# A shifted-window attention block: the value projection over all 128 rows in two column tiles, the output projection 128 columns wide

## The chip, the cores and the metric

The kernel runs on one core of one Trainium2 chip. The metric is device microseconds of one execution, start to end. A run of the program is timed as a whole; the profile is one further execution under the hardware profiler.

## What is computed

One Swin block on an input of 32 x 56 x 56 pixels with C = 64 channels, 8 heads of D = 8, windows of 7 x 7 = 49 tokens, shifted by 3:

```python
y = roll(layernorm(x), (-3, -3)); win = windows(y)                # (2048, 49, 64)
q, k, v = (win @ qkv_w.T).reshape(..., 3, 8, 8)
attn = softmax(q @ k.T * D**-0.5 + bias[head] + mask)
out = (attn @ v) @ proj_w.T + proj_b                              # per window
x = x + roll(windows_back(out), (3, 3))
x = x + gelu(layernorm(x) @ fc1_w.T + fc1_b) @ fc2_w.T + fc2_b    # hidden 256
```

The relative-position bias is made on the chip once, from a small network; everything is float32 at the boundary.

## The kernel before, in words

**Units.** The image is cut into 128 super-blocks (`NSB`). One holds 16 windows: 8 positions along the free axis (`UP`), each with two windows, one on partitions 0 to 48 and one on 64 to 112 (`W0 = 64`, `R = 113`). A round of the pipeline, `body(i)`, works on one super-block at each stage: while the scores of block i are made, block i+1 gets its projections, block i-1 its output projection, block i-3 its hidden layer, and so on.

**The order.** There is no scheduler. Each engine has its own `body(i, m)`, and the order in it is written by hand. Semaphores tie them. A round on TensorE has eight steps k = 0 to 7. Each step has the same core: `scores` (line 723, with 727 where a mask applies), `scores_T` (739), `shift` (745) and `times_v` (759). One extra piece is put between `scores_T` and `shift` (or at the end of the step):

- k = 0: `turn_back` (862), then `project_qk` (785)
- k = 1: `project_v` (801)
- k = 2 and 3: the two halves of `fc1` (832)
- k = 4: `turn_y` (767), then `fc2` (854)
- k = 5: `turn_o` (767); k = 6: `project_out` (818); k = 7: `turn_z` (767)

VectorE, ScalarE and GpSimd run their loops as a hardware loop of four rounds. TensorE's program is written out in full for all 135 rounds (`for i in range(-3, NSB + 4)` at its end), so it is one long straight piece of code.

**Operands.** `yT` holds the normalised tokens transposed: partitions 0 to 63 are the 64 channels of the even positions, 64 to 127 those of the odd ones (index h). The weights lie in both halves (`twice`), so that each half of the rows has its own copy. `M` is four PSUM banks of 512 float32 columns.

**`project_v(u)`** (line 796) makes 32 matmuls: for each of 8 token groups s, for both row halves h and both head parities e, stationary `yT[64 rows, 49 columns]`, moving `wv[64 rows, 32 columns]`. The four go to four quarters of the array, `tile_position=(C * h, W0 * e)`, and write bank 2 + h. A float32 matmul is executed as two MATMULs with two weight loads, so the trace counts 64. ScalarE's `place_v` (line 421, activation at 428) copies both banks into `vx`, the ring of values that `times_v` reads by a window index (line 756).

**`project_out(u, f)`** (line 811) makes 8 matmuls: for each q of 4 and each row half h, stationary `oT[64 rows, 113 columns]`, moving `wproj[64 rows, 64 columns]`, output bank h. VectorE's `add_attention` (606, 610) adds both banks to the residual.

**Start.** VectorE fills the PSUM tiles S, ST and O (505 to 507); TensorE waits for these three (`BLANK`, line 693), and then for the constants' chain on VectorE.

Of the kernel before, what the change touches and what calls it, by code (L numbers as in the profile page):

```python
# [14 lines left out]
N = WIN * WIN  # L15
SHIFT = 3
HEADS = 8
D = 8
C = HEADS * D
HID = 4 * C  # L20
PAIRS = 4
W0 = 64
R = W0 + N
# [11 lines left out]
EPS = 1e-5  # L35
U = 8
NVEC = 23 + SPAN
NWT = 768
RING = 4
LAG = 4  # L40
FIRST = 7
# [2 lines left out]
def swin_block(nc, x, c_vec, c_weights, c_projb, c_keys, c_diag, c_shift, out):  # L44
    NSB = x.shape[0]
    ctx = ExitStack()
    with ctx:
        def sb(name, shape, dt=F32):
            return ctx.enter_context(nc.sbuf_tensor(name, shape, dt))

        def ps(name, shape):
            return ctx.enter_context(nc.psum_tensor(name, shape, F32))

        def sem(name):
            return ctx.enter_context(nc.semaphore(name))

        vec = sb("vec", [128, NVEC])
        weights = sb("weights", [128, NWT])
        diag = sb("diag", [RM, 2 * 4, N], F16)
# [8 lines left out]
        line = vec[:, 23:23 + SPAN]  # L68
        ident = weights[:, 0:128]
        wqk = weights[:, 128:256]  # L70
        wproj = weights[:, 256:320]
        w1 = weights[:, 320:576]
        wv = weights[:, 576:640].rearrange("c (e f) -> c e f", e=2)
        w2 = weights[:, 640:768].rearrange("k (a c) -> k a c", a=2)

        st = sb("st", [128, 12, 4])
        tab = sb("tab", [128, 8, SPAN])
# [18 lines left out]
        yT = sb("yT", [2 * C, UT // 2])  # L96
# [3 lines left out]
        vx = [sb(f"vx{r}", [R, 16, 4, VC]) for r in range(RING)]  # L100
# [3 lines left out]
        pT = [sb(f"pT{n}", [R, 2, 4, N]) for n in range(LAG)]  # L104
        rec = sb("rec", [R, 4 * PAIRS, 2])
        on = sb("on", [R, UP, C])
        oT = sb("oT", [2 * C, 4, R])
# [19 lines left out]
        M = ps("M", [128, 4, 512])  # L127
# [6 lines left out]
        c_blank = sem("c_blank")  # L134
# [56 lines left out]
        s_out = [sem(f"s_out{r}") for r in range(2)]  # L191

        ZEROED = RING + 2
        BLANK = 3
        VALUES = 3 * RING

        C_EXP, C_BASE, C_HID = 2, 10, 19
# [1 line left out]
        def on_chip(u):  # L199
            return not isinstance(u, int) or 0 <= u < NSB  # L200

        def later(u, k=1):
            return not isinstance(u, int) or u >= k
# [191 lines left out]
        def _(act):  # L395
# [25 lines left out]
            def place_v(u, r):  # L421
                act.wait_ge(s_vp, u + 1)
                if not later(u, RING):
                    act.wait_ge(c_values, 3 * u + 3)
                dst = vx[r % RING][:].rearrange("n s h f -> n (s h) f")
                for e in range(2):
                    rows = slice(W0 * e, W0 * e + N)
                    nc.scalar.activation(dst[rows, :, D * e:D * e + D].rearrange("n (a s) d -> n a s d", a=2),  # L428
                                         M[rows, 2:4, 0:256].rearrange("n a (s d) -> n a s d", d=D),
                                         ACT.Copy).then_inc(s_vx, 1)  # L430

            def exp(u, j):
# [33 lines left out]
            def body(i, m):  # L466
                a, n, c, d, e = i + 1, i + 3, i - 1, i - 2, i - 3
                if isinstance(i, int) and i == 0:
                    place_bias(0, 1)
                    act.wait_ge(c_zero, ZEROED)  # L470
                for k in range(U):
                    if isinstance(i, int) and i == 0 and k in (5, 7):
                        place_bias(1, k // 7)
                    if k == 0 and on_chip(a):
                        high_parts(a)
                    if k == 1 and on_chip(a):
                        place_v(a, m + 1)
                    u, j = at_unit(i, k, 2)
                    if on_chip(u):
                        exp(u, j)  # L480
                    if k == 0 and on_chip(d):
                        square2(d)
                    if k == 2 and on_chip(e):
                        gelu(e, 0)
                        gelu(e, 1)
                    if k == 3 and on_chip(n):
                        square1(n)
                    if k == 4 and on_chip(c):
                        evac_oT(c)
                    if k == 5 and on_chip(e):  # L490
                        evac_m(e)
# [4 lines left out]
        def _(dve):  # L496
# [7 lines left out]
            V = nc.vector  # L504
            V.memset(S[:], -1.0).then_inc(c_blank, 1)
            V.memset(ST[:], 0.0).then_inc(c_blank, 1)
            V.memset(O[:], 1.0).then_inc(c_blank, 1)
            dve.wait_ge(c_vec_in, 16)

            then(V.scalar_tensor_tensor(st[:, 0, 0:3], scal[:, 0:3], -1.0, scal[:, 0:3], ALU.mult, ALU.max))  # L510
# [95 lines left out]
            def add_attention(u, r):  # L606
                dve.wait_ge(s_pj, u + 1)
                dve.wait_ge(s_xres, u + 1)
                held = xres[r % RING][:].rearrange("r (p h) c -> r p h c", h=2)
                V.tensor_tensor(held, M[0:R, 0:2, 0:4 * C].rearrange("r h (p c) -> r p h c", c=C), held,  # L610
                                ALU.add).then_inc(s_att, 1)

            def ln2_sum(u, r):
# [33 lines left out]
            def body(i, m):  # L647
# [5 lines left out]
                for k in range(U):  # L653
# [29 lines left out]
                    if k == 6 and on_chip(c):  # L683
                        add_attention(c, m + 3)
# [4 lines left out]
        def _(pe):  # L689
            MM = nc.tensor.matmul  # L690

            pe.wait_ge(c_vec_in, 16)
            pe.wait_ge(c_blank, BLANK)
            pe.wait_ge(c_chain, C_HID)
            for n in range(HALF + 1):
                for half in range(2):
                    kr, kc = divmod(HALF * half + n if n else 0, WIN)
                    dst = S[:] if n < 10 else ST[:, n // 10 - 1, :]
                    mm = MM(dst[W0 * half:W0 * half + HEADS, N * (n % 10):N * (n % 10) + N], cpbw2,
                            hidden[:, kr:kr + WIN, kc:kc + WIN], start=True, stop=True, tile_position=(0, W0 * half))  # L700
# [48 lines left out]
            def times_v(u, r, j):  # L749
                p = j % 4  # L750
                pe.wait_ge(s_e, U * u + j + 1)
                if j == 0:
                    pe.wait_ge(s_vx, 2 * u + 2)
                if p == 0 and (later(u) or j == 4):
                    pe.wait_ge(s_on, 2 * u + j // 4)
                window = 8 * (j % 2) + 4 * (j // 4) + 2 * ((j % 4) // 2)
                for hp in range(4):
                    for w in range(2):
                        mm = MM(O[W0 * w:W0 * w + N, (4 * p + hp) * VC:(4 * p + hp + 1) * VC],  # L759
                                pT[j % LAG][:, w, hp, :], vx[r % RING][:, window + w, hp, :],  # L760
                                start=True, stop=True, tile_position=(0, W0 * w))
                mm.then_inc(s_pv, 1)

# [31 lines left out]

            def project_v(u):
                for s in range(8):
                    for h in range(2):
                        for e in range(2):
                            rows = slice(C * h, C * h + C)  # L800
                            mm = MM(M[W0 * e:W0 * e + N, 2 + h, 32 * s:32 * s + 32], yT[rows, N * s:N * s + N],  # L801
                                    wv[rows, e, :], start=True, stop=True, tile_position=(C * h, W0 * e))
                mm.then_inc(s_vp, 1)

            def turn_o(u, e, a):
# [5 lines left out]
            def project_out(u, f):  # L811
                pe.wait_ge(s_oT, u + 1)
                if on_chip(f):
                    pe.wait_ge(s_yT, f + 1)
                for q in range(4):
                    for h in range(2):
                        rows = slice(C * h, C * h + C)
                        mm = MM(M[0:R, h, C * q:C * q + C], oT[rows, q, :], wproj[rows, :], start=True, stop=True)  # L818
                mm.then_inc(s_pj, 1)

            def turn_z(u, e, a):
# [44 lines left out]
            def body(i, m):  # L866
# [6 lines left out]
                for k in range(U):  # L873
# [14 lines left out]
                    if k == 1 and on_chip(a):  # L888
                        project_v(a)
# [8 lines left out]
                    if k == 6 and on_chip(c):  # L898
                        project_out(c, f)
# [4 lines left out]
                    if on_chip(u4):  # L904
                        times_v(u4, r4, j4)
# [87 lines left out]
```

## Time and profile before

| | |
|---|---|
| median of 3 runs | 2359.13 us (2358.63 to 2376.8) |
| the profiled execution | 2345.75 us, of which the span of the instructions is 2343.9 us |
| TensorE busy (matmul) | 2217.1 us, 95% of the span |
| mean granted TensorE clock | 0.986 |
| rounds | 128 full ones |

How to read it: in the lines of a group, "M<-weights,yT 64*49 64x32 f32" is a MATMUL that writes M, with a stationary operand of 64 rows by 49 columns and a moving one of 64 rows by 32 columns. PE is TensorE's matmul side, PEld its weight loads, which run beside it. Matmuls are pipelined: their durations overlap, so the time that a group takes is read from its start to the start of the next group. "[0.39 <-issue]" is idle time that nothing in the profile released: no semaphore that another engine set late. All starts are microseconds from the first instruction.

### The profile page before, as it was taken

The page shows a single profiled execution, that of the slowest core. Times are in us where ns is not written, and L with a number is a line of the kernel's source. Part 1 is how long each engine was busy: PE and PEld are TensorE (multiplying, and loading weights), DVE is VectorE, ACT ScalarE, POOL GpSimd, SP SyncE. Part 2 cuts the span into 40 slices and gives each one's busy share as a digit, 9 for nine tenths or more (in the row PEclk, how much of TensorE's full clock was granted, in tenths as well). Part 3 has the DMA queues.
Part 4 walks back from the last instruction along what each step waited for, and adds up shares of the span by engine and source line. Part 5 has one row for each costly group of instructions (what it writes and reads, how often), then busy time and mean ns, then how long its engine had stood idle before and what let it go on. Part 6 is the DMA issues. An engine that isn't in the chain of part 4 may idle for free.

```text
span 2343.9 us, 155989 instructions
## 1 busy us (share of the span) xinstructions
PE 2217.1 (95%) x66852; PEld 1699.0 (72%) x66852; DVE 1756.3 (75%) x3230; ACT 1548.0 (66%) x2435; POOL 1770.1 (76%) x1687
## 2 busy tenths in 40 slices
PE   5999999999999999999999999999999999999997
PEld 4777777777777777777777777777677777777775
DVE  5787787777777877777777777777777777777774
ACT  4567666666666776766666766666666666666765
POOL 5787787777777877776777777777777777777774
PEclk7999999999999999999999999999999999999999
DMA  5444444444444454444444444444444444444541
GB/s 122 98 92 103 91 94 100 87 90 90 95 97 90 96 100 90 99 90 85 96 87 92 102 89 93 103 93 90 94 90 89 93 91 97 94 91 93 103 87 41
DMA packets 137659, 217.73 MB, mean 93 GB/s; under 512 B 29336, under 2 KB 95114, under 8 KB 137114
## 3 DMA queue, kind: packets, MB, share of 16 engines
q1 hardware_dynamic: 137114, 208.95, 43.2%
q8 instruction: 527, 8.63, 1.7%
q14 instruction: 18, 0.15, 0.0%
HBM read 131.69 MB, written 77.15 MB: 89 GB/s over the span
## 4 chain that ended last, share of the span: by engine, by line
PE 85%; ACT 6%; issue 5%; DMA 1%; DVE 1%; POOL 0%; SPq 0%; ACTq 0%; POOLq 0%; DVEq 0%
PE O L759 13%; PE ST L745 11%; PE S L723 9%; PE M L767 9%; PE ST L739 8%; PE M L832 7%; PE M L854 7%; PE M L818 5%; PE M L785 5%; PE M L801 5%; PE M L862 3%; ACT L456 3%; ACT gl L456 2%; PE S L727 2%; DMA xin<-in_x 0%
## 5 line engine op out<-in xcount | busy, mean ns | idle before, releaser
L337 POOL TENSOR_TENSOR nmd<-diag,nm 121x392 f16<-121x392 f16 x1024 | 897.4, 885 | 435.6 <-DVE nm L592 412.5
L592 DVE TENSOR_REDUCE nm<-S 121x8 f16<-121x392 f32 x1024 | 576.7, 563 | 375.9 <-PE S L727 185.0
L437 ACT ACTIVATE pT<-ST 113x392 f32<-113x392 f32 x1024 | 506.2, 495 | 404.7 <-PE ST L745 400.2
L759 PEld LDWEIGHTS O<-vx,pT 113*49 113x49 f32 x16384 | 552.1, 127 | 61.1 <-issue 20.5
L759 PE MATMUL O<-vx,pT 113*49 113x18 f32 x16384 | 530.7, 197 | 16.7 <-issue 14.3
L723 PE MATMUL S<-kp,qp 128*49 128x49 f16 x16384 | 395.6, 186 | 26.4 <-issue 10.7
L739 PE MATMUL ST<-qp,kp 128*49 128x49 f16 x16384 | 396.8, 186 | 23.7 <-issue 22.7
L723 PEld LDWEIGHTS S<-kp,qp 128*49 128x49 f16 x16384 | 318.3, 104 | 100.3 <-issue 75.7
L745 PE MATMUL ST<-nmd,shiftw 121*49 121x392 f16 x2048 | 362.6, 350 | 2.0 <-POOL nmd L337 1.3
L739 PEld LDWEIGHTS ST<-qp,kp 128*49 128x49 f16 x16384 | 330.1, 103 | 37.5 <-issue 27.9
L745 PEld LDWEIGHTS ST<-nmd,shiftw 121*49 121x49 f16 x2048 | 107.1, 101 | 286.4 <-issue 150.0
L418 ACT ACTIVATE hl<-M 128x784 f16<-128x784 f32 x128 | 105.4, 823 | 268.7 <-PE M L785 268.7
L357 POOL TENSOR_TENSOR xres<-xin,projb 113x512 f32<-113x512 f32 x128 | 204.7, 1599 | 91.6 <-DVE res L644 85.6
L832 PE MATMUL M<-zT,weights 64*128 64x392 f32 x1024 | 245.0, 550 | 7.5 <-issue 5.7
L456 ACT ACTIVATE gl<-M,vec 128x784 f32<-128x784 f32 x256 | 220.4, 911 | 4.9 <-PE M L832 3.3
L364 POOL TENSOR_TENSOR rstd<-veps,mhalf 113x8 f32<-113x8 f32 x128 | 210.8, 1647 | 12.2 <-DVE veps L631 12.2
L344 POOL TENSOR_TENSOR rstd<-veps,mhalf 113x8 f32<-113x8 f32 x128 | 209.7, 1639 | 10.9 <-DVE veps L572 10.9
L854 PE MATMUL M<-gl,weights 128*64 128x392 f32 x1024 | 193.7, 500 | 4.3 <-ACT gl L456 4.3
L428 ACT ACTIVATE vx<-M 49x512 f32<-49x512 f32 x256 | 154.9, 605 | 27.8 <-PE M L801 18.1
L456 ACT ACT_TABLE_LOAD x126 | 161.7, 1283 | 2.2
L437 ACT ACT_TABLE_LOAD x126 | 161.7, 1283 | 2.2
L598 DVE RECIPROCAL rec<-O 113x32 f32<-113x32 f32 x256 | 90.3, 353 | 82.1 <-PE O L759 82.1
(87 smaller groups left out, 3297.6 us busy)
## 6 DMA issues: line engine op xcount, KB each, us to landing
parts<-hl SPq DMA_DIRECT2D x512, 98.0 KB, 2.6
qp<-parts SPq DMA_DIRECT2D x512, 98.0 KB
xin<-in_x SPq DMA_DIRECT2D x256, 98.0 KB
kp<-parts SPq DMA_DIRECT2D x256, 98.0 KB
kp<-parts SPq DMA_DIRECT2D x512, 49.0 KB
out<-res SPq DMA_DIRECT2D x256, 98.0 KB
kp<-in_c_keys SPq DMA_DIRECT2D x4, 588.0 KB, 8.4
weights<-in_c_weights SPq DMA_DIRECT2D x1, 384.0 KB, 3.6
```

The costliest lines, as they stand in the source:

```text
L337: nc.gpsimd.tensor_tensor(nmd[j % LAG][:], diag[:], nm[j % LAG][:].unsqueeze(2).broadcast_to([RM, 2 * 4, N]), ALU.mult).then_inc(s_nmd, 1)
L364: nc.gpsimd.tensor_tensor(rstd2[:], veps2[:], mhalf[:], ALU.pow).then_inc(s_rs2, 1)
L437: nc.scalar.activation(pT[j % LAG][:].rearrange("k w h q -> k (w h q)"), ST[0:R, j % 2, 0:HK], ACT.Exp).then_inc(s_e, 1)
L456: nc.scalar.activation(gl[:, c], M[:, 2 * c:2 * c + 2, 0:HT], ACT.Gelu, bias=b1[:, c:c + 1]).then_inc(s_g, 1)
L592: V.tensor_reduce(nm[j % LAG][:], S[0:RM, 0:HK].rearrange("q (h n) -> q h n", n=N), AX_X, ALU.max, negate=True).then_inc(s_nm, 1)
L723: mm = MM(S[W0 * e:W0 * e + N, N * (4 * w + hp):N * (4 * w + hp + 1)], q[:, 2 * hp + e, t], key[:, 2 * hp + e, t], start=(w == 0 and hp == ...
L739: MM(ST[W0 * e:W0 * e + N, j % 2, N * (4 * w + hp):N * (4 * w + hp + 1)], key[:, 2 * hp + e, t], q[:, 2 * hp + e, t], start=(w == 0 and hp ...
L745: mm = MM(ST[W0 * e:W0 * e + N, j % 2, 0:HK], shiftw[:, variant(r, j), e, :], nmd[j % LAG][:].rearrange("r h n -> r (h n)"), start=False, ...
L759: mm = MM(O[W0 * w:W0 * w + N, (4 * p + hp) * VC:(4 * p + hp + 1) * VC], pT[j % LAG][:, w, hp, :], vx[r % RING][:, window + w, hp, :], sta ...
L767: mm = nc.tensor.transpose(M[:, bank, 2 * W0 * q:2 * W0 * q + R], tokens[:, 2 * C * q:2 * C * q + 2 * C], ident[0:R, 0:R])
L832: mm = MM(M[:, 2 * c + h, 0:HT], w1[rows, 128 * c:128 * c + 128], zT[rows, :], start=True, stop=True)
L854: mm = MM(M[C * h:C * h + C, 2, 0:HT], w2[:, c, :], gl[:, c, h, :], start=(c == 0), stop=(c == 1), tile_position=(0, C * h), skip_group_ch ...
```

## The change

`project_v` uses all 128 rows at once. Its moving operand becomes 64 columns, of which the half that belongs to the other row half is zero (`apart` builds it): 16 matmuls instead of 32, in two column tiles (0 and 64), all into bank 2. `project_out` likewise: 4 matmuls instead of 8, moving operand 128 columns, all into bank 0. `place_v`, `add_attention` and the window index in `times_v` follow the new layout; M is also filled with zeros once at the start.

```diff
-NWT = 768
+NWT = 896
...
-        BLANK = 3
+        BLANK = 4
...
-                    nc.scalar.activation(dst[rows, :, D * e:D * e + D].rearrange("n (a s) d -> n a s d", a=2),
-                                         M[rows, 2:4, 0:256].rearrange("n a (s d) -> n a s d", d=D),
+                    nc.scalar.activation(dst[rows, :, D * e:D * e + D],
+                                         M[rows, 2, :].rearrange("n (s d) -> n s d", d=D),
                                          ACT.Copy).then_inc(s_vx, 1)
...
+            V.memset(M[:], 0.0).then_inc(c_blank, 1)
...
-                V.tensor_tensor(held, M[0:R, 0:2, 0:4 * C].rearrange("r h (p c) -> r p h c", c=C), held,
+                V.tensor_tensor(held, M[0:R, 0, :].rearrange("r (p h c) -> r p h c", h=2, c=C), held,
                                 ALU.add).then_inc(s_att, 1)
...
-                window = 8 * (j % 2) + 4 * (j // 4) + 2 * ((j % 4) // 2)
+                window = 8 * (j // 4) + 4 * ((j % 4) // 2) + j % 2
...
             def project_v(u):
                 for s in range(8):
-                    for h in range(2):
-                        for e in range(2):
-                            rows = slice(C * h, C * h + C)
-                            mm = MM(M[W0 * e:W0 * e + N, 2 + h, 32 * s:32 * s + 32], yT[rows, N * s:N * s + N],
-                                    wv[rows, e, :], start=True, stop=True, tile_position=(C * h, W0 * e))
+                    for e in range(2):
+                        mm = MM(M[W0 * e:W0 * e + N, 2, C * s:C * s + C], yT[:, N * s:N * s + N], wv[:, e, :],
+                                start=True, stop=True, tile_position=(0, W0 * e))
                 mm.then_inc(s_vp, 1)
...
                 for q in range(4):
-                    for h in range(2):
-                        rows = slice(C * h, C * h + C)
-                        mm = MM(M[0:R, h, C * q:C * q + C], oT[rows, q, :], wproj[rows, :], start=True, stop=True)
+                    mm = MM(M[0:R, 0, 2 * C * q:2 * C * q + 2 * C], oT[:, q, :], wproj, start=True, stop=True)
                 mm.then_inc(s_pj, 1)
...
+    def apart(a):
+        a = np.asarray(a).reshape(C, -1, a.shape[-1])
+        both = np.zeros((2, C, a.shape[1], 2, a.shape[2]), np.float32)
+        both[0, :, :, 0], both[1, :, :, 1] = a, a
+        return both.reshape(2 * C, -1)
```

Where the value projection stands on TensorE, step k = 1 of a round in the middle, before (a "x32" counts matmuls as written; M<-weights,yT is the projection):

```order
L723 MATMUL S<-kp,qp 49x49 x16
L739 MATMUL ST<-qp,kp 49x49 x16
L801 MATMUL M<-weights,yT 49x32 x32
L745 MATMUL ST<-nmd,shiftw 49x392 x2
L759 MATMUL O<-vx,pT 49x18 x8
```

The same place of the changed kernel:

```order
L724 MATMUL S<-kp,qp 49x49 x16
L740 MATMUL ST<-qp,kp 49x49 x16
L800 MATMUL M<-weights,yT 49x64 x16
L746 MATMUL ST<-nmd,shiftw 49x392 x2
L760 MATMUL O<-vx,pT 49x18 x8
```

Nothing changed places; the step has 16 matmuls fewer, each twice as wide.

The output projection on TensorE, step k = 6, before (M<-weights,oT):

```order
L739 MATMUL ST<-qp,kp 49x49 x16
L818 MATMUL M<-weights,oT 113x64 x8
L745 MATMUL ST<-nmd,shiftw 49x392 x2
L759 MATMUL O<-vx,pT 49x18 x8
L723 MATMUL S<-kp,qp 49x49 x16
```

And in the changed kernel:

```order
L740 MATMUL ST<-qp,kp 49x49 x16
L815 MATMUL M<-weights,oT 113x128 x4
L746 MATMUL ST<-nmd,shiftw 49x392 x2
L760 MATMUL O<-vx,pT 49x18 x8
L724 MATMUL S<-kp,qp 49x49 x16
```

Again the place is the same, with half as many matmuls, each twice as wide. On VectorE one MEMSET of M, 128 x 2048, comes fourth in the program, ahead of the constants' chain.

## Rows read from the trace of the kernel before

**Rows 1.** The page, part 1: busy time of each engine
```profile
PE 2217.1 (95%) x66852; PEld 1699.0 (72%) x66852; DVE 1756.3 (75%) x3230; ACT 1548.0 (66%) x2435; POOL 1770.1 (76%) x1687
```
**Rows 2.** The page, part 4: the chain that ended last, by engine
```profile
PE 85%; ACT 6%; issue 5%; DMA 1%; DVE 1%; POOL 0%; SPq 0%; ACTq 0%; POOLq 0%; DVEq 0%
```
**Rows 3.** TensorE in order of time, pieces of one round: start, us from first start to last end, group
```profile
1221.14 1.51 PE L854 MATMUL M<-gl,weights 128*64 128x392 f32 x8
1222.49 0.37 PE L723 MATMUL S<-kp,qp 128*49 128x49 f16 x16
...
1224.59 1.01 PE L818 MATMUL M<-weights,oT 64*113 64x64 f32 x16
1225.53 0.35 PE L745 MATMUL ST<-nmd,shiftw 121*49 121x392 f16 x2
...
1227.38 0.51 PE L759 MATMUL O<-vx,pT 113*49 113x18 f32 x16
1227.82 0.69 PE L862 MATMUL M<-weights,mT 128*113 128x128 f32 x4
1228.44 0.39 PE L723 MATMUL S<-kp,qp 128*49 128x49 f16 x16
...
1230.88 0.94 PE L801 MATMUL M<-weights,yT 64*49 64x32 f32 x64
1231.75 0.35 PE L745 MATMUL ST<-nmd,shiftw 121*49 121x392 f16 x2
```
**Rows 4.** The same view of line 862, once cut after two and once after three matmuls
```profile
1227.82 0.47 PE L862 MATMUL M<-weights,mT 128*113 128x128 f32 x2
1227.82 0.58 PE L862 MATMUL M<-weights,mT 128*113 128x128 f32 x3
```
**Rows 5.** Line 818 in two stretches: stretch, its length, PE busy (count), clock, DMA
```profile
1224.50:1224.70 0.20, 0.11 (x2) 1.00 0.56 94
1224.50:1225.10 0.60, 0.51 (x10) 1.00 0.55 84
```
**Rows 6.** TensorE in order of time, from one idle on issue to past the next
```profile
1247.96 0.37 PE L739 MATMUL ST<-qp,kp 128*49 128x49 f16 x15 [0.89 <-issue]
1248.26 0.93 PE L785 MATMUL M<-yT,weights 64*128 64x392 f32 x4
1249.12 0.35 PE L745 MATMUL ST<-nmd,shiftw 121*49 121x392 f16 x2
1249.31 0.51 PE L759 MATMUL O<-vx,pT 113*49 113x18 f32 x16
1249.66 0.37 PE L723 MATMUL S<-kp,qp 128*49 128x49 f16 x16
1249.87 0.38 PE L739 MATMUL ST<-qp,kp 128*49 128x49 f16 x16
1250.17 0.92 PE L801 MATMUL M<-weights,yT 64*49 64x32 f32 x58
1252.09 0.29 PE L801 MATMUL M<-weights,yT 64*49 64x32 f32 x6 [1.00 <-issue]
...
1256.39 0.51 PE L759 MATMUL O<-vx,pT 113*49 113x18 f32 x16
...
1257.55 0.29 PE L767 MATMUL M<-weights,y 113*128 113x113 f32 x1 [0.23 <-ACT gl L456]
```
**Rows 7.** The page, part 3: the DMA queue that brings instructions (fetches, MB, share)
```profile
q8 instruction: 527, 8.63, 1.7%
```
**Rows 8.** TensorE's groups with idle on issue, 100 to 2290 us: first and last of 100
```profile
104.95 0.29 PE L723 MATMUL S<-kp,qp 128*49 128x49 f16 x8 [0.66 <-issue]
...
2287.08 0.93 PE L832 MATMUL M<-zT,weights 64*128 64x392 f32 x3 [0.86 <-issue]
```
**Rows 9.** A stretch behind an idle: busy us of PE, PEld, DVE, ACT, POOL, clock, DMA
```profile
1028.00:1048.00 20.00, 19.72 (x509) 14.60 (x511) 11.88 (x22) 11.33 (x18) 11.72 (x12) 0.83 0.35 75
```
**Rows 10.** VectorE's start: the last memset before the chain of the constants
```profile
2.54 0.48 DVE L507 MEMSET O<- 128x512 f32 x1
```

More of the change, by code:

```diff
@@ L70, in swin_block @@
         wqk = weights[:, 128:256]
[L71 to L74, printed above, removed]
+        wproj = weights[:, 256:384]
+        w1 = weights[:, 384:640]
+        wv = weights[:, 640:768].rearrange("c (e f) -> c e f", e=2)
+        w2 = weights[:, 768:896].rearrange("k (a c) -> k a c", a=2)
         st = sb("st", [128, 12, 4])
@@ L759, in times_v @@
                         mm = MM(O[W0 * w:W0 * w + N, (4 * p + hp) * VC:(4 * p + hp + 1) * VC],
-                                pT[j % LAG][:, w, hp, :], vx[r % RING][:, window + w, hp, :],
+                                pT[j % LAG][:, w, hp, :], vx[r % RING][:, window + 2 * w, hp, :],
                                 start=True, stop=True, tile_position=(0, W0 * w))
@@ L972 @@
                every(L0_conv_h_times, L0_conv_ws_scalar, L0_conv_ws_scalar2, L0_conv_pow_para), every(line)]
-    matrices = [ident, twice(qkv[0:2].transpose(3, 0, 2, 1)), twice(np.asarray(L0_conv_proj_w).T),
-                twice(np.asarray(L0_conv_fc1_w).T), twice(qkv[2].reshape(4, 2, D, C).transpose(3, 1, 0, 2)),
+    matrices = [ident, twice(qkv[0:2].transpose(3, 0, 2, 1)), apart(np.asarray(L0_conv_proj_w).T),
+                twice(np.asarray(L0_conv_fc1_w).T),
+                apart(qkv[2].reshape(4, 2, D, C).transpose(3, 1, 0, 2).reshape(C, 2, C // 2)),
                 fc2_wT.reshape(128, 2 * C)]
```

## The prediction, made before the changed kernel was run

> **What bounds the kernel now.** I began with the busy shares on the page: TensorE 95%, no other engine over 76% [rows 1]. The chain that ended last agrees: 85% of it is TensorE's own work, and 5% is "issue", time in which nothing that the profile shows held TensorE back [rows 2]. So TensorE's straight program sets the time, and two things can change it: how long its groups take, and those idle moments.
>
> For the first I read TensorE in order of time, from the start of a group to the start of the next [rows 3]. Line 854 has four pairs of column tiles over 392 columns: 1222.49 - 1221.14 = 1.35 us, 0.338 a pair. In line 862 (128 rows, 128 columns) a third matmul adds 0.58 - 0.47 = 0.11 us [rows 4]. In line 818, eight more matmuls, four row-tile pairs, add 0.51 - 0.11 = 0.40 us, 0.10 a pair [rows 5]. Line 759, eight pairs of 18 columns, takes 1249.66 - 1249.31 = 0.35 us, 0.044 a pair [rows 6].
>
> For the second I looked at what stands between two idles on issue [rows 6]. From 1247.96 to the idle before 1252.09 there are 15 + 4 + 2 + 16 + 16 + 16 + 58 = 127 matmuls, 254 instructions with their weight loads. The page has an instruction queue with 527 fetches [rows 7], and TensorE executed 2 x 66852 = 133704 such instructions [rows 1]: 254 a fetch. So the idle is TensorE at the end of a fetched block with the next not there. This block took 1252.09 - 1.00 - 1247.96 = 3.1 us of work and then waited 1.0; the next 127 matmuls end inside the group at 1256.39, some 4.3 us on, and no issue idle stands there. A block must last about 4 us, or TensorE waits for instructions. The value projection is what makes blocks short: 64 matmuls in 0.94 us [rows 3], nearly half a block.
>
> Counted over 100 to 2290 us, the view has 100 idles on issue, 62.8 us in all [rows 8]. By place: 70 of them, 46.7 us, lie between the start of the value projection and the end of the second step behind it; the other 30, 16.1 us, in the remaining five and a half steps of the eight. The largest are also followed by half clock: the 20 us behind one of 2.1 us ran at a mean granted clock of 0.83 [rows 9], which is a part of the stretch at the lower level, 1.2 GHz.
>
> **The change part by part.**
>
> *Value projection.* Before: 1231.75 - 1230.88 = 0.87 us [rows 3], and the group starts 0.30 behind the group before it, where two groups in column tiles follow each other in 0.21 [rows 6]: 0.96 us with the entry. After, there are 16 pairs of 64 columns, 128 rows. No row shows 64 columns there. Below it is line 759's 0.044 a pair, 0.70 us in all; above it 128 columns' 0.11, 1.76 us. Between 128 and 392 columns the slope is (0.338 - 0.11) / 264 = 0.86 ns a column, so 64 columns take 0.11 - 0.055 = 0.055 us. That clears the 0.044 which 49-column weight loads seem to set. 16 x 0.055 = 0.88, and since its neighbours work in the same column tiles I leave 0.04 for entry and exit: 0.92. Gain 0.04 x 128 rounds = 5 us; the ends give -33 and +102.
>
> The row shows 0.09 us of extra entry for the quartered layout. The Trainium skill, TensorEngine Tiling (Array Packing), section Key Properties, says that a change of tiling mode, not just of tile, drains the engine. By that rule this entry goes away with the row halves, as I took it; without it the gain would be nothing.
>
> *Output projection.* Before: 1225.53 - 1224.59 = 0.94 us [rows 3]. After: 8 executed matmuls of 128 rows, 113 stationary and 128 moving columns, exactly the shape of line 862, at 0.11. That group takes 1228.44 - 1227.82 = 0.62 for four, so 0.18 beyond 4 x 0.11 for going in and out. 8 x 0.11 + 0.18 = 1.06 us; the entry gap itself stays, as both layouts differ from their neighbours'. Loss 0.12 x 128 = 15 us. Here the two row halves ran at once and cost 0.10 a pair, so nothing is saved by merging them. Ends: 0, if it keeps 0.10 and its present entry; +118 if each load (0.10) stood in line with its stream (0.11): 8 x 0.21 + 0.18 = 1.86.
>
> *Blocks of instructions.* Per round 32 + 8 = 40 executed matmuls and as many loads go, 10240 instructions of 133704: some 40 fetches fewer. More important, the densest step becomes 50 + 32 = 82 matmuls in about 2 us instead of 114, and 127 matmuls around it reach into the next step's long group: about 3.6 us, near the 4 that a block must last, where now it is 2.1 to 3.1. I expect the idles near the value projection to fall from 46.7 to about 9 us, the rate of the other steps (16.1 / 5.5 x 2.5 = 7) and a little more. That is 38 us in 2190, 40 over the whole. Of this I give back 5: before line 767 TensorE waits 0.23 us for gelu on ScalarE [rows 6], and an idle ahead of that point now swallows the wait. Fewer deep idles also mean less half clock; 5 us. Ends: 0, if the idles only move; -63 and some 10 more for the clock, if nearly all go.
>
> *The rest.* The memset of M is four times the 0.48 us of O's [rows 10] and ahead of the constants' chain at the start: +2 us. `place_v` and `add_attention` handle as many elements as before, from one bank instead of two, on ScalarE (66% busy) and VectorE (75%) [rows 1]: nothing, since TensorE covers them; if the copies grew by a tenth, ScalarE would still have a third of its time free. The window index is only an address. 64 KB more weights are loaded at the start, beside the constants' chain: nothing.
>
> Sum: -5 + 15 + 2 - 40 + 5 - 5 = -28 us. The profiled execution had 2345.75 us, 13 below the median of the runs, 2359.13; the sum goes onto the median: 2331 us, 1.2% faster. (2318 for a profiled execution like the one shown.)
>
> **The rivals.**
>
> *The idles stay (2371 us).* If a block is late for a reason that hardly depends on its length, say the fetch waits behind the kernel's own transfers, only the arithmetic of the groups counts: -5 + 15 + 2 = +12 us, 0.5%. For it: 30 idles lie in steps with long groups, too. Against it: 70 of 100 lie behind the value projection, and in the example the block of 3.1 us waited while the next, of 4.3 us, did not.
>
> *Nearly all idles go (2298 us).* 12 - 63 - 10 = -61. For it: the shortest block grows past most that wait now. Against: the 16 us elsewhere, whose blocks hardly change.
>
> *Slower: loads no longer beside the streams (2504 us).* Row halves let a weight load for one half run while the other half streams; with all 128 rows each load might stand in line. Value projection: 16 x (0.044 + 0.055) = 1.58 against 0.96; output projection 1.86 against 0.94. Together 1.54 us a round, +197; with +2, and with denser blocks gone entirely, so -54 for idles: 2504. It decides from 0.069 us a pair in the value projection on (28 / 128 / 16 above 0.055). Line 862 speaks against it: 0.11 us a matmul at 128 rows [rows 4], with a load of the same 113 columns that paces line 818 at 0.10. In the Trainium skill, TensorE: Matmul & The Clock Gate, section The mechanism, a rule says that a load overlaps matmuls in flight only when its row group differs; by that rule this rival would be the forecast. The row of line 862 contradicts it, so I give it little.
>
> **How the numbers follow.** Forecast (some 2315 to 2347): 0.55. Idles stay wholly or mostly (2347 to 2374): 0.22. Nearly all go (2290 to 2315): 0.15. Slower by loads or by another price of the groups: 0.08. The range from 2297 to 2375 leaves out the slow rival and half of the best one. A measurement of this kernel can tell about 1% from no change, 24 us here. The line is at 2335.5: of the forecast's 0.55 about 0.39 lies below it, with 0.15 of the second rival 0.54 for faster; 0.08 for slower; 0.38 between.
>
> **What would show it.** In the changed kernel's profile: 61732 matmuls instead of 66852; value projection 0.92 us start to start with 32 in it and entry at 0.21 to 0.24 behind the group before; output projection 1.06 with 8; some 487 instruction fetches; idles on issue between 100 and 2290 us near 25 us instead of 62.8, and no longer heaped behind the value projection; TensorE's clock up by about half a hundredth. I am wrong on the main point if the idles stay near 60 us or if a pair of 64 columns costs more than 0.06 us.

## The result, and the profile after

| | before | changed |
|---|---|---|
| median of 4 runs | 2358.88 us (2346.61 to 2376.8) | 2268.25 us (2266.34 to 2271.25) |
| profiled execution | 2345.75 us | 2268.08 us |
| mean granted TensorE clock | 0.986 | 0.992 |

Ratio 0.9611, interval 0.9548 to 0.9674: 3.9% faster, where 1.2% was forecast and the range ended at 2297 us. The direction was right, the size was not. The runs of the changed kernel also lie within 5 us of each other, those of before within 30.

The page of the changed kernel, busy time of each engine:

```profile
PE 2186.6 (96%) x61732; PEld 1685.1 (74%) x61732; DVE 1748.9 (77%) x3231; ACT 1548.1 (68%) x2435; POOL 1770.5 (78%) x1687
```

and its instruction queue:

```profile
q8 instruction: 487, 7.98, 1.6%
```

Both are as forecast: 5120 executed matmuls fewer than in [rows 1] and 40 fetches fewer than in [rows 7]. TensorE is still the bound.

TensorE in order of time in the changed kernel (start, us from first start to last end, group):

```profile
1219.65 1.13 PE L815 MATMUL M<-weights,oT 128*113 128x128 f32 x8
1220.71 0.35 PE L746 MATMUL ST<-nmd,shiftw 121*49 121x392 f16 x2
...
1225.76 0.37 PE L740 MATMUL ST<-qp,kp 128*49 128x49 f16 x16
1225.98 1.08 PE L800 MATMUL M<-weights,yT 128*49 128x64 f32 x32
1226.89 0.33 PE L746 MATMUL ST<-nmd,shiftw 121*49 121x392 f16 x2
```

Read from start to start against [rows 3]. The output projection takes 1220.71 - 1219.65 = 1.06 us, forecast 1.06, before 0.94. The value projection takes 1226.89 - 1225.98 = 0.91, and it starts 0.22 behind the group before it instead of 0.30. (The 1.08 behind its start is not its price: it is where the last matmul ends, and the next group begins before that.) So both groups cost what was forecast. One of the two is slower than before and the other hardly faster.

A quiet round, from one value projection to the next with no wait for instructions between, shows the sum. Before the change, two that follow each other:

```profile
691.60 0.94 PE L801 MATMUL M<-weights,yT 64*49 64x32 f32 x64
...
708.51 0.94 PE L801 MATMUL M<-weights,yT 64*49 64x32 f32 x64
```

and in the changed kernel:

```profile
1242.94 1.08 PE L800 MATMUL M<-weights,yT 128*49 128x64 f32 x32
...
1259.91 1.08 PE L800 MATMUL M<-weights,yT 128*49 128x64 f32 x32
```

16.91 us before, 16.97 after (17.29 and 17.37 in the one round of four that has six masked matmuls more). The kernel's own work became 0.06 us a round longer, 8 us in all, plus the memset:

```profile
3.40 1.76 DVE L508 MEMSET M<- 128x2048 f32 x1 [0.38 <-issue]
```

TensorE's first matmul starts at 13.86 us instead of 11.72, 2.1 us later; 2 was forecast.

So the whole gain, and 10 us more, comes out of the waits. TensorE's waits between 100 and 2200 us, before the change (waited for: us in total, times, longest):

```profile
PE ST L739 <- issue: 21.9, 29, 2.1
PE O L759 <- issue: 13.7, 19, 2.1
PE M L767 <- ACT gl L456: 12.3, 55, 0.2
PE S L723 <- issue: 10.2, 26, 1.2
PE M L801 <- issue: 5.6, 8, 1.0
PE M L832 <- issue: 4.9, 6, 1.1
PE M L767 <- issue: 2.7, 4, 1.2
...
PE M L818 <- issue: 1.1, 3, 0.6
```

and in the changed kernel:

```profile
PE M L768 <- ACT gl L456: 19.1, 83, 0.5
PE ST L740 <- issue: 6.5, 12, 1.0
PE O L760 <- issue: 3.1, 3, 1.5
PE S L724 <- issue: 1.0, 3, 0.4
PE M L815 <- issue: 0.2, 1, 0.2
```

With the small groups, issue fell from 61.4 us in 98 waits to 10.8 in 19, while the wait for gelu rose from 12.3 to 19.1. Part of that is the cover that an idle used to give: in the trace of before, rounds without an idle on issue waited 0.14 us for gelu on the mean, rounds with one 0.09. So 7 us came back where 5 were expected. (It isn't in proportion: in less_dma below, issue halved and this wait only rose to 13.1.) In the stretch of [rows 9] the changed kernel has the full clock, 1.00 instead of 0.83, and 51 matmuls more, though it needs fewer of them:

```profile
1028.00:1048.00 20.00, 19.77 (x560) 15.60 (x562) 15.84 (x30) 13.92 (x24) 16.53 (x17) 1.00 0.51 101
```

One measure is used below for all kernels: "above quiet", the mean length of a round less its quiet length (for each matmul the median distance to the next over all like rounds, summed up). It holds the waits for instructions with all they bring, and the half clock, and leaves the groups' own price out. Before it was 0.83 us a round, after 0.17. (0.83 - 0.17) x 128 = 84 us less, against 8 + 2 us more. That makes -74 of the -78 us between the two profiled executions. By the medians of the runs the kernel gained 91 us, since the profiled execution of before was 13 us faster than its median; the waits then gave some 100.

### The profile page after: what moved, and what is told of

Its sections match the earlier page's. It is cut to its first block, busy times and chain, and to the rows that moved or that the text cites. A ratio compares the mean times of both kernels' runs of the same rounds, so it can differ in the third digit from the quotient of the medians.

```text
span 2266.3 us, 145750 instructions
## 1 busy us (share of the span) xinstructions
PE 2186.6 (96%) x61732; PEld 1685.1 (74%) x61732; DVE 1748.9 (77%) x3231; ACT 1548.1 (68%) x2435; POOL 1770.5 (78%) x1687
## 4 chain that ended last, share of the span: by engine, by line
PE 83%; ACT 9%; issue 4%; DVE 1%; POOL 1%; DMA 1%; SPq 0%; ACTq 0%; DVEq 0%; POOLq 0%
PE O L760 13%; PE ST L746 11%; PE M L768 9%; PE S L724 9%; PE ST L740 8%; PE M L851 8%; PE M L829 6%; PE M L815 6%; PE M L800 5%; PE M L786 5%; ACT L456 4%; ACT gl L456 4%; PE M L859 3%; PE S L728 1%; DMA xin<-in_x 0%
## 5 line engine op out<-in xcount | busy, mean ns | idle before, releaser
L760 PEld LDWEIGHTS O<-vx,pT 113*49 113x49 f32 x16384 | 545.9, 126 | 47.2 <-issue 7.2
L760 PE MATMUL O<-vx,pT 113*49 113x18 f32 x16384 | 521.1, 196 | 4.5 <-issue 3.6
L724 PE MATMUL S<-kp,qp 128*49 128x49 f16 x16384 | 387.8, 186 | 14.1 <-DMA kp<-parts 9.1
L740 PE MATMUL ST<-qp,kp 128*49 128x49 f16 x16384 | 388.2, 185 | 9.1 <-issue 8.4
L724 PEld LDWEIGHTS S<-kp,qp 128*49 128x49 f16 x16384 | 313.2, 104 | 85.1 <-issue 63.0
L740 PEld LDWEIGHTS ST<-qp,kp 128*49 128x49 f16 x16384 | 324.3, 103 | 18.1 <-issue 10.0
L829 PE MATMUL M<-zT,weights 64*128 64x392 f32 x1024 | 237.5, 540 | 1.6 <-DVE zT L638 1.6
L364 POOL TENSOR_TENSOR rstd<-veps,mhalf 113x8 f32<-113x8 f32 x128 | 210.8, 1647 | 12.3 <-DVE veps L632 12.3
L344 POOL TENSOR_TENSOR rstd<-veps,mhalf 113x8 f32<-113x8 f32 x128 | 209.8, 1639 | 10.9 <-DVE veps L573 10.9
L611 DVE TENSOR_TENSOR xres<-M,xres 113x512 f32<-113x512 f32 x128 | 88.5, 691 | 92.8 <-PE M L815 92.8
```

Of the source, the lines that this page charges most:

```text
L344: nc.gpsimd.tensor_tensor(rstd1[:], veps1[:], mhalf[:], ALU.pow).then_inc(s_rs1, 1)
L364: nc.gpsimd.tensor_tensor(rstd2[:], veps2[:], mhalf[:], ALU.pow).then_inc(s_rs2, 1)
L724: mm = MM(S[W0 * e:W0 * e + N, N * (4 * w + hp):N * (4 * w + hp + 1)], q[:, 2 * hp + e, t], key[:, 2 * hp + e, t], start=(w == 0 and hp == ...
L740: MM(ST[W0 * e:W0 * e + N, j % 2, N * (4 * w + hp):N * (4 * w + hp + 1)], key[:, 2 * hp + e, t], q[:, 2 * hp + e, t], start=(w == 0 and hp ...
L829: mm = MM(M[:, 2 * c + h, 0:HT], w1[rows, 128 * c:128 * c + 128], zT[rows, :], start=True, stop=True)
```

## The experiments

Ten kernels, each timed in three rounds beside the kernel before. "Block" is the quiet time of 127 executed matmuls, worked out from the quiet round and its 481 to 521 matmuls. "Above quiet" comes from the one profiled execution; the column beside it is the same figure moved by the distance from that execution to the median of all runs of the kernel, divided by 128 rounds.

| kernel | us | ratio to before (interval) | block, us | above quiet, us a round | by the median | issue 100 to 2200 us | clock |
|---|---|---|---|---|---|---|---|
| before | 2359 (2351 to 2353 in the experiments) | | 4.14 | 0.83 | 0.88 to 0.93 | 61.4 | 0.986 |
| spread | 2361.19 | 1.0019 (0.9984 to 1.0054) | 4.20 | 0.73 | 0.68 | 48.0 | 0.975 |
| out_only | 2346.91 | 0.9979 (0.9946 to 1.0011) | 4.24 | 0.64 | 0.71 | 55.5 | 0.991 |
| thin_even | 2332.28 | 0.9907 (0.9870 to 0.9943) | 4.30 | 0.27 | 0.33 | 21.5 | 0.992 |
| thin_one | 2359.48 | 1.0020 (0.9988 to 1.0052) | 4.33 | 0.37 | 0.42 | 31.7 | 0.991 |
| pad_one | 2366.19 | 1.0064 (1.0030 to 1.0098) | 4.37 | 0.25 | 0.32 | 20.9 | 0.993 |
| v_only | 2274.18 | 0.9672 (0.9615 to 0.9729) | 4.40 | 0.36 | 0.33 | 23.7 | 0.988 |
| changed | 2268.25 | 0.9611 (0.9548 to 0.9674) | 4.50 | 0.17 | 0.17 | 10.8 | 0.992 |
| no_memset | 2264.14 | 0.9621 (0.9581 to 0.9661) | 4.50 | 0.12 | 0.13 | 10.9 | 0.993 |
| pad_even | 2464.29 | 1.0476 (1.0431 to 1.0520) | 4.62 | 0.08 | 0.12 | 3.6 | 0.993 |
| less_dma | 2296.76 | 0.9779 (0.9722 to 0.9836) | 4.14 | 0.43 | 0.45 | 33.7 | 0.995 |
| after_less_dma | 2250.71 | 0.9564 (0.9525 to 0.9602) | 4.50 | 0.02 | 0.05 | 1.1 | 0.996 |

How far to trust that measure: changed and no_memset have the same TensorE program and differ by 0.04 to 0.05 us. A difference of 0.1 is near the limit, and below, such differences are read from both columns.

**v_only: the value projection alone.** The kernel with the new `project_v`, the old `project_out`, no memset.

```diff
             def project_out(u, f):
...
-                    mm = MM(M[0:R, 0, 2 * C * q:2 * C * q + 2 * C], oT[:, q, :], wproj, start=True, stop=True)
+                    for h in range(2):
+                        rows = slice(C * h, C * h + C)
+                        mm = MM(M[0:R, h, C * q:C * q + C], oT[rows, q, :], wproj[rows, :], start=True, stop=True)
```

> Only the value projection is changed (16 wide matmuls, two column tiles, all 128 rows); the output projection keeps its 8 matmuls of 64 columns, and the memset of M is left out. Theory A (the gain is TensorE not waiting for its next block of instructions, because the densest step got thinner): nearly the whole gain of the change is here, and the output projection's +0.12 us a round (15 us) and the memset's 2 us are saved on top: 2268 - 17 = about 2251 us, with at most 5 us lost again to a few more idles; idles on issue from 100 to 2200 us between 11 and 20 us. Theory B (half of the gain is from merging the output projection, by its shorter program): about 2300 us, with idles near 35 us.

Measured 0.9672. Most of the gain is here, as theory A has it, and theory B is out. But the 17 us on top did not come: 2251 us would be a ratio of 0.957, below the interval. The issue waits are 23.7 us, above the 11 to 20 expected. Its output projection takes what it took before:

```profile
1307.68 1.01 PE L816 MATMUL M<-weights,oT 64*113 64x64 f32 x16
1308.62 0.35 PE L745 MATMUL ST<-nmd,shiftw 121*49 121x392 f16 x2
```

0.94 us. So the 0.12 us were saved, and 0.36 - 0.17 = 0.19 us a round of waiting came back for them (0.16 by the medians). The trace shows where. Between the start of the value projection and the end of the second step behind it, idles on issue fell from 46.7 us to 6.4. In the other steps they did not fall at all: 18.6 us in 25 idles, where the kernel before had 16.1 in 30. In step k = 6, that of the output projection, there were 16.1 us, before 9.2, and in the changed kernel 5.8.

**out_only: the output projection alone.** The kernel before with the new `project_out` (the changed lines of it in the diff of the change, `add_attention` with them).

> Only the output projection is changed (4 matmuls of 128 columns); the value projection keeps its 32 matmuls in four quarters. Theory A: nothing in the dense step changes, so the idles stay near 60 us and the time is that of before plus 8 x 0.11 + 0.18 - 0.94 = 0.12 us a round: 2359 + 15 = 2374 us, a few us less if the 16 executed instructions fewer a round take some idles away. Theory B: about 2320 us.

Measured 0.9979: not 15 us slower, the interval ends at 1.0011 and 2374 us would be 1.0064. Its output projection does take 1.06 us:

```profile
1314.41 1.13 PE L816 MATMUL M<-weights,oT 128*113 128x128 f32 x8
1315.47 0.35 PE L745 MATMUL ST<-nmd,shiftw 121*49 121x392 f16 x2
```

Again the round's own work grew and the time above quiet fell, by 0.83 - 0.64 = 0.19 us (0.18 by the medians). From both sides the 16 instructions (8 matmuls and 8 loads) fewer a round in step k = 6, far from the value projection, are worth 0.16 to 0.19 us of waiting, some 20 to 24 us in all. Of that the idles themselves show little, 59.1 us against 62.8 between 100 and 2290 us: near the value projection they stayed at some 47 us, elsewhere they fell from 16.1 to 11.6. A part is the slower clock behind them: the granted clock, averaged over all runs, was 0.989, that of before beside it 0.983, which is worth up to 14 us. That the waiting falls with a step that isn't dense spoke against theory A, in which only the densest step counts.

**spread: the same instructions, in two steps.**

```diff
-            def project_v(u):
-                for s in range(8):
+            def project_v(u, part):
+                for s in range(4 * part, 4 * part + 4):
...
-                mm.then_inc(s_vp, 1)
+                if part == 1:
+                    mm.then_inc(s_vp, 1)
...
-                    if k == 1 and on_chip(a):
-                        project_v(a)
+                    if k in (1, 2) and on_chip(a):
+                        project_v(a, k - 1)
```

and on ScalarE `place_v` in step 2 instead of 1.

> The kernel before with the same instructions, but the value projection in two halves of 16 matmuls, one in step k = 1 and one in step k = 2; ScalarE copies the values in step 2. The number of instructions and fetches stays that of before. Theory A (what counts is how many instructions stand in a few us): the densest step has 82 executed matmuls instead of 114, so idles fall to between 15 and 35 us; two more changes of array layout and a copy 0.2 us later for the exponentials cost up to 0.4 us a round. Sum about 2359 - 55 + 35 = 2339 us (2310 to 2360). Theory C (what counts is the total number of instructions or of fetches): idles stay near 60 us and the time rises to 2375 to 2410 us.

Measured 1.0019, issue 48.0 us: between the theories. The quiet round grew by 0.22 us, 28 us, for two more changes of layout, and the waiting took about as much off again: 0.10 us a round in the profiled execution, which was slower than the median and has the lowest clock of all, 0.975; 0.20 by the medians. Halving the dense group helped, but by far less than v_only's 0.47 (0.56 by the medians).

**less_dma: fewer transfers of the kernel's own.** From the third super-block on, three of the five reloads of the query and key parts are left out.

```diff
+                if later(u, 2):
+                    return
                 sp.dma_start(q[BIAS + 2 * D:BIAS + 4 * D], both[0]).then_inc(landed, 16)
...
-                    pe.wait_ge(s_q[r % 2][b], 80 * (u // 2) + 80)
+                    pe.wait_ge(s_q[r % 2][b], 32 * (u // 2) + 80)
```

> The kernel before, without three of the five reloads of the query and key parts from the third super-block on (those rows keep the values of the first two), a quarter of the kernel's own DMA traffic. Theory A in its plain form (a fetch takes its time whatever else is moved): idles stay at 55 to 65 us, time 2355 to 2360 us. Theory D (a block is late because its fetch stands behind the kernel's own transfers): idles fall by a quarter to a half, time 2310 to 2340 us.

Measured 0.9779, 56 us off; issue 33.7 instead of 61.4 us. That is theory D, with a gain larger than its 2310 to 2340 us allowed. TensorE's program is the same 66852 matmuls and its quiet round the same. Only the traffic beside the fetches changed. The stretch from 500 to 2000 us, before and then less_dma; the last two numbers are the busy share of the DMA engines and GB/s:

```profile
500.00:2000.00 1500.00, 1441.15 (x43494) 1104.41 (x43495) 1137.85 (x2086) 1005.27 (x1587) 1147.88 (x1086) 0.99 0.45 93
```

```profile
500.00:2000.00 1500.00, 1461.95 (x44794) 1123.54 (x44796) 1167.55 (x2148) 1035.66 (x1633) 1181.59 (x1118) 1.00 0.30 73
```

With a share of 0.30 instead of 0.45 TensorE gets 1300 matmuls more done in the same 1500 us. The idles away from the value projection nearly went, from 16.1 to 3.5 us. So how late a block of instructions comes depends on what else the DMA engines carry. The single records of the instruction queue say how: a fetch itself hardly changed (1.22 us on the mean before, 1.17 here), but it started sooner, 0.94 us instead of 1.15 behind the start of the block before it (medians; the block starts between two idles are interpolated).

**after_less_dma: the same edit on the changed kernel.**

> The changed kernel without three of the five reloads of the query and key parts from the third super-block on (those rows keep the values of the first two). Before the change this took 56 us off, by shorter waits for instructions. If a late fetch is the same cause in both kernels, the changed one has only 0.17 us a round left to give: 2248 to 2260 us. If taking the transfers away helps by another way (scores waiting for their keys), it takes some 50 us off here too: about 2215 us.

Measured 2250.71 us, 18 us below the changed kernel's median and 13 below no_memset, which ran beside it. That is what a late fetch allows (0.17 - 0.02 = 0.15 us a round, 19 us) and far from 50. The two remedies work on one and the same loss, and issue is down to 1.1 us. This kernel is also the ceiling: without waits for instructions the changed work takes about 2250 us.

**pad_one and pad_even: instructions given back.** Into `times_v` of the changed kernel go tiny matmuls whose results nobody uses, 32 executed a round; the diff is of pad_even, and pad_one has `range(8 if j == 5 else 0)`.

```diff
+                for n in range(1):
+                    for w in range(2):
+                        mm = MM(O[W0 * w:W0 * w + 8, 300:308], pT[j % LAG][:, w, 0, 0:8],
+                                vx[r % RING][:, window + 2 * w, 0, 0:8], start=True, stop=True, tile_position=(0, W0 * w))
                 mm.then_inc(s_pv, 1)
```

> The changed kernel with 16 tiny matmuls more a round (8 x 8, two column tiles, results unused; 32 executed), all in step k = 1, beside the value projection: that step has 114 executed matmuls again, as before the change. In quiet rounds each pair should cost 0.02 to 0.03 us, 0.3 to 0.5 us a round. From the six runs so far, a round's time above its quiet time was 0.83 us (before, 4.15 us of quiet time a block of 127 matmuls), 0.73 (spread, 4.20), 0.64 (out_only, 4.24), 0.36 (v_only, 4.41), 0.17 (changed, 4.51). Theory C (only the mean length of a block counts): about 4.3 us a block, so 0.45 to 0.6 us a round above the quiet time, the same as in pad_even. Theory A (the densest step counts): 0.7 us or more a round, clearly above pad_even.

> The changed kernel with the same 16 tiny matmuls a round, two in each of the eight steps. Theory C: as pad_one, 0.45 to 0.6 us a round above its quiet time. Theory A: little more than the changed kernel, 0.17 to 0.35 us.

The price was misjudged. Eight stationary columns put the array into another layout, and going in and out costs as much as the work: in pad_even four of them take 1301.89 - 1301.76 = 0.13 us, and start 0.09 later than a group without a change would:

```profile
1301.32 0.51 PE L760 MATMUL O<-vx,pT 113*49 113x18 f32 x16
1301.76 0.21 PE L765 MATMUL O<-vx,pT 113*8 113x8 f32 x4
1301.89 0.39 PE L724 MATMUL S<-kp,qp 128*49 128x49 f16 x16
```

The quiet round of pad_even grew by 1.6 us, so its blocks are long, 4.62 us, and nearly nothing is left above quiet (0.08), less than either theory said. pad_one with 114 executed matmuls in step 1 again had only 0.25, below theory C's 0.45 to 0.6 and far below theory A's 0.7. Both expectations missed, and the pair doesn't compare like with like, but pad_one alone already speaks against theory A.

**thin_one and thin_even: the same, without the change of layout.** 32 small float16 matmuls a round of 49 stationary columns, all in one step or four in each.

```diff
+                for n in range(16 if j == 5 else 0):
+                    for w in range(2):
+                        mm = MM(O[W0 * w:W0 * w + N, 300:308], shiftw[:, 0, 0, :], diag[:, 0, 0:8],
+                                start=True, stop=True, tile_position=(0, W0 * w))
                 mm.then_inc(s_pv, 1)
```

(thin_even has `range(2)`.)

> The changed kernel with 32 small float16 matmuls more a round (49 stationary columns, 8 moving, results unused), all behind times_v in step k = 1. They keep the array layout of their neighbours, so unlike in pad_one and pad_even no change of layout blurs the price: 16 pairs at 0.022 to 0.027 us, 0.35 to 0.45 us a round, 45 to 58 us in all. Step k = 1 has 114 executed matmuls again, in some 2.4 us. Theory C (the mean length of a block counts: here 17.07 + 0.4 us over 512 / 127 = 4.03 blocks, 4.33 us): 0.35 to 0.5 us a round above the quiet time, the same as in thin_even; both about 2268 + 50 + 30 = 2348 us. Theory A (the densest step counts): 0.6 us or more a round above the quiet time here, 2370 us or more.

> The same 32 small float16 matmuls a round, four in each of the eight steps. Theory C: as thin_one, 0.35 to 0.5 us a round above its quiet time, about 2348 us. Theory A: little above the changed kernel's 0.17 us a round, about 2320 to 2330 us, with waits for instructions near 15 us.

In thin_one the 32 take 1308.21 - 1307.78 = 0.43 us, at the end of the value projection's step:

```profile
1307.26 0.33 PE L746 MATMUL ST<-nmd,shiftw 121*49 121x392 f16 x2
1307.43 0.51 PE L760 MATMUL O<-vx,pT 113*49 113x18 f32 x16
1307.78 0.57 PE L765 MATMUL O<-diag,shiftw 121*49 121x8 f16 x32
1308.21 0.37 PE L724 MATMUL S<-kp,qp 128*49 128x49 f16 x16
```

Above quiet: 0.37 us in one step, 0.27 spread out, 0.17 with neither (0.42, 0.33, 0.17 by the medians); issue 31.7, 21.5 and 10.8 us. thin_one fell into theory C's range and thin_even below it, into theory A's. More instructions bring waits even where they are spread evenly (+0.10 to +0.16), and bunching them adds some 0.1 more. Neither theory A nor theory C holds alone. Of the 27 us between the two kernels, some 13 are this waiting, with an uncertainty of about 7; the other 14 are the quiet round, 17.51 against 17.39 us. That part has another cause: thin_one still waits 15.3 us for gelu between 100 and 2200 us, thin_even not once, as some of its spread matmuls fill that gap.

**no_memset: the changed kernel without the fill of M.**

> The changed kernel without the memset of M at the start. The chain at the start should be 2.1 us shorter, as line 700 began 2.1 us later with it; nothing else changes: 2266 us, the same as the changed kernel within what is measurable.

Measured 2264.14 us; its ratio's interval covers that of the changed kernel. Nothing measurable, as expected.

## Why the prediction was wrong in size

Point by point, by its own steps. What failed is one term, "Blocks of instructions": its idles were under-priced, and the output projection was given no part in it.

*What bounds the kernel.* Right: TensorE's program and the moments when it waits for its next block of instructions. That the wait is for instructions is now more than an argument: with the program and the groups' times unchanged, it shrank by half when only other transfers were taken away (less_dma). And the trace of before shows the fetches themselves. From 1249.20 to 1252.10 us, around the block that ended in the idle of 1.0 us in [rows 6], the instruction queue has one:

```profile
q8 instruction: 1, 0.02, 2.9%
```

It ran from 1249.27 to 1250.60 us (2.9% of 16 engines over 2.9 us is 1.3 us on one engine), and TensorE's next matmul started at 1252.09, 1.5 us after it. It is so for all 100 idles of [rows 8]: each ends 1.2 to 1.9 us after the end of a fetch, median 1.45, where a moment taken at random lies 0.2 to 4.4 us behind one. All 99 distances from idle to idle are multiples of 127 matmuls, to within five. The fetches before these idles began between 0.1 us ahead of the start of the block before and 3.4 us behind it.

The rule "a block must last about 4 us" was too simple. It came from one pair of blocks. Of the 100 idles of before, 44 stand behind blocks with under 3.2 us of work, but 24 behind blocks with over 4.1, and the 20 that the changed kernel has left stand behind 3.7 to 5.9 us. What a block must cover is the start of the fetch, late by 0 to 3 us, the fetch of 0.9 to 1.8 us, and the 1.2 to 1.9 us behind it.

*Value projection, -5 us; output projection, +15 us; memset, +2 us.* Right: 0.91 us for a forecast 0.92, 1.06 for 1.06, 2.1 us for 2. A pair of 64 columns costs 0.91 / 16 = 0.057 us, where the line through the rows of 128 and 392 columns gave 0.055. The layout's entry went away where the neighbours use the same column tiles (0.22 instead of 0.30) and stayed for the output projection.

*Blocks of instructions, -40 us, with +5 and -5.* This is the term that failed; it measured about -84 between the profiled executions and some -100 by the medians. v_only splits it. The value projection gave (0.83 - 0.36) x 128 = 61 us, the output projection 23.

First, the output projection. The prediction gave its shorter program no part in this term and took the idles away from the value projection as fixed: "the rate of the other steps". For the value projection alone that was right. v_only has 25.0 us of idles on issue between 100 and 2290 us, as forecast: 6.4 near it, where about 9 were forecast, and 18.6 elsewhere, where all 16 were to stay. The changed kernel has 20 idles, 11.5 us, where [rows 8] closed a list of 100 and 62.8. The first and the last:

```profile
136.38 0.18 PE L740 MATMUL ST<-qp,kp 128*49 128x49 f16 x1 [1.04 <-issue]
...
2205.01 0.34 PE L740 MATMUL ST<-qp,kp 128*49 128x49 f16 x13 [0.75 <-issue]
```

Of these 3.7 us are near the value projection and 7.9 elsewhere. So what fell elsewhere, 18.6 to 7.9 us, fell with the output projection's 16 instructions. v_only and out_only both give them 0.16 to 0.19 us a round: more than the 0.12 us that they cost. The merged output projection was priced as a plain loss of 15 us; by these figures it is a gain of some 5 to 9. That it isn't a loss of 15 is clear (the interval of out_only ends at 1.0011); that it is a gain isn't clear of noise, as the intervals of v_only and of the changed kernel overlap and that of out_only holds 1.

Second, an idle was priced by its shown length. Before the change, in order of time:

```profile
1231.93 0.41 PE L759 MATMUL O<-vx,pT 113*49 113x18 f32 x11
1232.73 0.31 PE L759 MATMUL O<-vx,pT 113*49 113x18 f32 x5 [0.39 <-issue]
1232.85 0.39 PE L723 MATMUL S<-kp,qp 128*49 128x49 f16 x15
```

The group takes 1232.85 - 1231.93 = 0.92 us where a quiet one takes 0.35: 0.57 us lost, with 0.39 shown. Matmuls overlap, and the idle is counted only from the end of the last one, so each adds some 0.18 us; over 72 idles of before the median of this hidden part is 0.19. 80 idles fewer are 14 to 15 us.

Third, the slower clock. Between 100 and 2200 us the time at 1.2 GHz fell from 34 us to 7. For 27 us less, up to 14 us are given back, where 5 were assumed. This part varies from one execution to the next (v_only has 24 us, no_memset none), so its size is the least certain.

These add up, over the whole program: 55 us of shown idles less, 14 hidden, up to 14 of clock, and 7 back for gelu, -76 of the -84. The rest stays open; idles under 0.15 us are in no list.

*The rivals.* "Nearly all idles go" came nearest, at 2298 us; it had the right sign and still the shown length as the price. "The idles stay" and "loads no longer beside the streams" are out: a pair costs 0.057 us, under the 0.069 from which the latter decides. The rule of the Trainium skill that would have made it the forecast (TensorE: Matmul & The Clock Gate, The mechanism) doesn't hold by itself for these matmuls of 128 rows; 0.057 us a pair and 0.13 us a matmul (1.06 / 8, with the change of layout) leave no room for a load and a stream in line. The same section of the Trainium skill names a second case in which a load is pulled ahead, into a background weight buffer; no run here shows where the loads went.

What stays open is the law by which a block becomes late. The table's column above quiet falls with the length of a block from 0.83 us at 4.14 to 0.08 at 4.62, but not in strict order: thin_one lies above thin_even with blocks as long, and less_dma far below before. Why one fetch starts 3 us later than another no run separates. How far ahead TensorE fetches, the records above bound: the fetch that ended an idle had begun no earlier than 0.1 us ahead of the start of the block before it, so it was never two blocks ahead. The Trainium skill, Advanced Engine Details and Errata, section ISA Cache, gives lines of 16 KB, 256 instructions. The trace agrees with 254 a fetch, and 8.63 MB in 527 fetches. The section also says "Only 2 cache lines!", and beside it 128 KB for TensorE, which would be eight. The fetches here look like two: one block runs while the next comes.

## What to carry to other kernels

In a long straight TensorE program of small matmuls, count the instructions: 127 small matmuls with their loads made one fetch here. With blocks of 4.1 us on the mean, the shortest that waited at 2.3, TensorE waited 61 us of 2100 for them; with 4.5 us on the mean, 11. There, half as many matmuls of twice the width are worth it even if half of the operand is zeros and the group itself gets no faster. Idle on "issue" that comes back at multiples of 127 matmuls is the sign; price it by the distance from start to start, with the slower clock that follows it, and expect it to shrink when the kernel moves less data. Give every group that loses instructions its share of the idles, also one that gets slower by itself.

## What the runs showed of the hardware that was not expected

- A quarter less data moved by the kernel in a round (93 to 73 GB/s at the shorter rounds) took 56 us off a kernel that TensorE bounds, without touching TensorE's program.
- TensorE went on 1.2 to 1.9 us after the end of the fetch that it lacked (all 100 idles of before), and a fetch of 16 KB took 0.9 to 1.8 us there.
- 16 instructions a round, 1.5% of TensorE's, were worth 0.16 to 0.19 us of waiting in a round of 17.9 us, about 1%, by v_only and by out_only.
- Two column tiles over 128 rows with 64 moving columns in float32 cost 0.057 us a pair, against 0.87 / 16 = 0.054 for four quarters with 32 columns each: per group the four quarters had bought next to nothing, and their entry cost 0.08 us more (0.30 against 0.22).
- Matmuls of 8 stationary columns between matmuls of 49 cost a change of layout: 0.13 us for four of them and 0.09 before them, where 32 of 49 stationary columns in float16 take 0.43.
